# Cross-attention's product with the values, in 64-column blocks per head

## The reference, cut to what matters

```
x = x + xattn(layernorm(x), ctx)          # 64 batches x 64 queries, 256 keys each, 16 heads of 64
    q, k, v = x @ Wq, context @ Wk, context @ Wv
    sim  = einsum('bhid,bhjd->bhij', q, k) * SCALE
    attn = softmax(sim)
    out  = einsum('bhij,bhjd->bhid', attn, v)      # the product with the values
    return out @ Wo + bo
x = x + attn(layernorm(x))                # self-attention, causal
x = x + moe(layernorm(x))                 # 8 experts, top 2
```

## Time and profile before

| | |
|---|---|
| median of 3 runs | 2512.0 us (2511.35 to 2512.2) |
| the profiled execution, its own time | 2510.75 us |
| its span, first to last instruction | 2509.0 us, so 1.75 us lie around it |
| PE busy | 2347.6 us, 94% |
| PEld busy | 2076.7 us, 83% |
| DVE busy | 1589.8 us, 63% |
| ACT busy | 1314.9 us, 52% |
| POOL busy | 903.4 us, 36% |
| granted TensorE clock, mean | 0.978 |
| cross-attention | up to about 1366 us |
| self-attention | about 1405 to 2010 us |
| experts | the rest |

### The profile page before, as it was taken

The page is one execution under the profiler, slowest core; times in us unless marked ns, Lnnn a source line. Parts: engine busy times, 40 slices in busy tenths (PEclk is TensorE's granted clock), DMA queues, the critical chain, the costliest instruction groups (busy, mean ns, idle before and its releaser), DMA issues. The chain is left out here.

```text
span 2509.0 us, 49491 instructions
## 1 busy us (share of the span) xinstructions
PE 2347.6 (94%) x16096; PEld 2076.7 (83%) x16096; DVE 1589.8 (63%) x3452; ACT 1314.9 (52%) x3960; POOL 903.4 (36%) x1141
## 2 busy tenths in 40 slices
PE   6999999999999999999997999999999956888895
PEld 5898889888988898889886899999999844777775
DVE  5656665666566656665655788888888855334332
ACT  4555555555555555555554666666666622333332
POOL 3233333333233323333332122222222224777774
PEclk9999999999999999999999999999999986999998
DMA  5000000000000000000001000000000012334334
GB/s 166 18 10 17 8 17 8 17 9 16 8 17 14 11 8 17 16 9 9 16 1 66 3 10 18 17 8 17 17 8 17 18 37 67 77 73 97 72 49 97
DMA packets 52931, 73.89 MB, mean 29 GB/s; under 512 B 9408, under 2 KB 36800, under 8 KB 52800
## 3 DMA queue, kind: packets, MB, share of 16 engines
q1 hardware_dynamic: 39952, 55.07, 6.9%
q0 software_dynamic: 12912, 17.98, 4.4%
HBM read 55.47 MB, written 21.76 MB: 31 GB/s over the span
## 5 line engine op out<-in xcount | busy, mean ns | idle before, releaser
L356 POOL TENSOR_TENSOR p_sb<-p_sb,rinv 128x512 f32<-128x512 f32 x256 | 284.1, 1110 | 906.3 <-DVE rinv L606 906.3
L527 ACT ACTIVATE p_sb<-s_ps,nmax 128x256 f32<-128x256 f32 x512 | 238.3, 470 | 467.1 <-DVE nmax L587 441.4
L751 POOL TENSOR_TENSOR sp_sb<-sp_sb,srinv 128x512 f32<-128x512 f32 x128 | 133.4, 1042 | 442.7 <-DVE srinv L937 442.7
L462 PE MATMUL o_ps<-pt_sb,v_sb 128*128 128x128 f32 x2048 | 270.5, 275 | 1.8 <-DVE ot_lo L57 1.8
L58 DVE SCALAR_TENSOR_TENSOR qbd_lo<-m_ps,qbd_hi 64x256 fp32r<-64x256 f32 x256 | 108.1, 422 | 227.4 <-ACT qbd_hi L46 225.7
L462 PEld LDWEIGHTS o_ps<-pt_sb,v_sb 128*128 128x128 f32 x2048 | 248.7, 192 | 2.2 <-issue 2.2
L57 DVE TENSOR_TENSOR kt_lo<-k_ps,kt_hi 128x512 fp32r<-128x512 f32 x256 | 176.2, 688 | 98.1 <-ACT kt_hi L45 94.1
L45 ACT CAST kt_hi<-k_ps 128x512 fp32r<-128x512 f32 x256 | 150.6, 588 | 105.7 <-PE k_ps L65 102.7
L885 ACT ACTIVATE sp_sb<-sm_sb,snmax 128x128 f32<-128x128 f32 x512 | 199.4, 390 | 6.6 <-DVE snmax L948 3.3
L603 DVE COPY pt_sb<-t_ps 128x512 f32<-128x512 f32 x256 | 176.4, 689 | 26.5 <-PE t_ps L449 21.8
L587 DVE TENSOR_REDUCE nmax<-s_ps 128x2 f32<-128x512 f32 x256 | 174.1, 680 | 0.0
(11 more groups left out here) (278 smaller groups left out, 7711.3 us busy)
## 6 DMA issues: line engine op xcount, KB each, us to landing
ctx_raw<-in_ctx_t SPq DMA_DIRECT2D x32, 256.0 KB, 2.8
ctx_raw<-in_ctx_t SPq DMA_DIRECT2D x64, 128.0 KB, 2.9
xn<-f_xn SPq DMA_DIRECT2D x16, 256.0 KB, 2.2
acc<-x_sb SPq DMA_DIRECT2D x16, 256.0 KB, 2.3
e_raw<-in_gate SPq DMA_DIRECT2D x8, 512.0 KB, 4.1
e_raw<-in_up SPq DMA_DIRECT2D x8, 512.0 KB, 5.0
e_raw<-in_down SPq DMA_DIRECT2D x8, 512.0 KB, 6.3
x_sb<-in_x SPq DMA_DIRECT2D x1, 3584.0 KB, 13.6
```

The source lines that it names most:

```text
L356: nc.gpsimd.tensor_tensor(prob, prob, inv, ALU.mult).then_inc(norm_done, 1)
L462: mm = pe.matmul(o_ps[:, (2 * w + b) * P:(2 * w + b + 1) * P], v_sb[:, k, q * P:(q + 1) * P], pt_sb[:, w, k * P:(k + 1) * P], start=(j == ...
L527: ex = nc.scalar.activation(p_sb[:, k, b * J:(b + 1) * J], s_ps[1 - w][:, b * J:(b + 1) * J], ACT.Exp, bias=nmax[:, k, b:b + 1], scale=1.0 ...
L751: nc.gpsimd.tensor_tensor(prob, prob, inv, ALU.mult).then_inc(norm_done, 1)
```

## The change

Each of the four fp32 matmuls of a step becomes two, one per head h. The weights are that head's 64 columns of v_sb, the moving operand that head's 64 columns of pt_sb, and the result goes to that head's 64 partitions and to 64 columns of o_ps. The result is dense: two steps fill columns 0 to 255 of o_ps on all 128 partitions. ACT and DVE then read it with one instruction of 128 partitions each, `diag` goes away, and the counts on ot_hi_done follow.

```
-                                    mm = pe.matmul(o_ps[:, (2 * w + b) * P:(2 * w + b + 1) * P],
-                                                   v_sb[:, k, q * P:(q + 1) * P], pt_sb[:, w, k * P:(k + 1) * P],
-                                                   start=(j == 0), stop=(j == 1))
+                                    for h in range(2):
+                                        mm = pe.matmul(o_ps[h * HEAD:(h + 1) * HEAD, (2 * w + b) * HEAD:(2 * w + b + 1) * HEAD],
+                                                       v_sb[:, k, q * P + h * HEAD:q * P + (h + 1) * HEAD],
+                                                       pt_sb[:, w, k * P + h * HEAD:k * P + (h + 1) * HEAD],
+                                                       start=(j == 0), stop=(j == 1))
...
-            def diag(h, w):
-
-                r = slice(h * HEAD, (h + 1) * HEAD)
-                return o_ps[r, :].rearrange("p (k q) -> p k q", k=4)[:, :, h * HEAD:(h + 1) * HEAD]
-
-            def ot_part(ot, h, q):
-                r = slice(h * HEAD, (h + 1) * HEAD)
-                return ot[r, q - 1:q + 1, :].rearrange("p a (b q) -> p (a b) q", b=2)
+            def ot_part(ot, q):
+                return ot[:, q - 1:q + 1, :].rearrange("p a t -> p (a t)")
...
-                            for h in range(2):
-                                split_hi_act(nc, ot_part(ot_hi, h, (p - 4) % PAIRS), diag(h, w)).then_inc(ot_hi_done, 1)
+                            split_hi_act(nc, ot_part(ot_hi, (p - 4) % PAIRS), o_ps[:, 0:2 * P]).then_inc(ot_hi_done, 1)
...
-                            dve.wait_ge(ot_hi_done, PAIRS * t + p - 3)
+                            dve.wait_ge(ot_hi_done, PAIRS // 2 * t + (p - 3) // 2)
                             q = (p - 4) % PAIRS
-                            for h in range(2):
-                                lo = split_lo_dve(nc, ot_part(ot_lo, h, q), diag(h, w), ot_part(ot_hi, h, q))
-                            lo.then_inc(ot_done, 1)
+                            split_lo_dve(nc, ot_part(ot_lo, q), o_ps[:, 0:2 * P], ot_part(ot_hi, q)).then_inc(ot_done, 1)
```

## The result

The changed kernel takes 2471.5 us (median, 2470.0 to 2472.7) against 2512.1 us before, a ratio of 0.9837 with a 95% interval of 0.982 to 0.9854. That is 40.6 us less. The forecast was 2486 us, with bounds of 2475 to 2497, so the sign was right, the size was not, and the time lies under the lower bound.

What follows compares the result with a forecast made beforehand. Cross-attention was taken as bound by TensorE's own stream. Its shorter groups (-25.3 us) and the relief of ACT and DVE (-1 us) made -26 us, from a median of 2512.0 to 2486 us, bounds 2475 to 2497.

Steps and rivals of the forecast that it cites:

- Parts 1 and 2: Line 462, cross-attention: both heads' blocks run side by side as pairs; switching form at both group ends takes 0.505 us.
- Part 3: Line 462's stretch per step: 0.505 + 7 x 0.058 = 0.911 us, 0.099 less than before; -25.3 us over 256 steps.
- Part 4: Reading o_ps with fewer ACT and DVE instructions counts only where TensorE waits for them: -1 us, -5 at most.
- Part 5: TensorE reaches 58 places with a waiting load 0.1 us earlier, giving back up to 6 us; nothing was taken.
- A: Line 462: a floor per matmul makes 64-column pairs pace like 128-column ones; 2582 us, slower; 15 in 100.
- B: Line 462: short loads and matmuls don't overlap fully, pace 0.065 to 0.082 us; 2499 to 2530 us; 16 in 100.
- C: Group ends cost less, or ACT and DVE's relief removes the loads' waits: -35 to -45 us; 5 in 100.

Runs made afterwards that it cites:

- experiment 4: Changed kernel, but with 128 moving columns, the result in its old place and the old two instructions on ACT and DVE; 2568.9 us, ratio 1.0237 to before.
- experiment 5: Changed kernel, but batch 0's four matmuls issued ahead of the transposes and batch 1's behind, so two groups per step; 2539.4 us, ratio 1.0102 to before.
- experiment 6: Changed kernel, but products of two steps issued together in the odd steps, 128 groups instead of 256; 2440.5 us, ratio 0.9725 to before.
- experiment 1: Changed kernel, but ACT and DVE each read the dense result in two instructions of 64 partitions; 2495.1 us, ratio 0.9941 to before.

## Why the prediction was right or wrong

**What bounds the part.** "The stretch is bound by TensorE's own stream ... what ACT and DVE save is not on this path" was wrong. TensorE was busy for 98.9% of the stretch, but a busy time that is the union of overlapping, modelled records hides waits of up to 0.16 us each and shortens the longer ones. The lengths of the steps, 5.50 and 5.17 beside 5.08 and 4.36, were in the same trace and show 25 us of lateness where the waits of TensorE's matmuls add to under 10.

**Parts 1 and 2, pairs and switches.** Right in kind and in size. The pair is concurrent at 64 columns too, the pace is 0.0585 us for 0.058, the ends cost about what line 816's cost (experiments 4, 5 and 6). One sign failed: behind the group the loader's idle time is 0.07 us, not 0.17 to 0.19, though the next matmul comes nearly when it was forecast.

**Part 3, the sum.** Right in kind, a little large: a step lost 0.08 us, not 0.099, so 20.5 us, not 25.3. The stretch measures 0.925 us after, for 0.911 forecast: 0.003 of it is the pace, seven times 0.0005, and 0.011 the two ends. Before, it measures 1.007, read as 1.01. Of the 20.5 only 13.3 (alone) or 14.8 (with the readers' part) reached the end.

**Part 4, ACT and DVE.** This is the step that failed. It was sized at -1 us, "-5 at the very most", and measured 22.0 us on top of the blocks and 20.5 alone. DVE's part is 18.6 of the 22.0 and 19.6 of the 20.5, the rest lies in the drain. The busy time was right (54 us forecast as 53 on DVE), the claim about who waits for it was not. The gains of two places were capped by the idle time in the earlier trace rows, and the chain that makes those waits was not followed.

**Part 5, what is late next.** The +6 us for waits that a faster TensorE uncovers is borne out by experiment 1, where 7 of 20.5 us were lost so. But "between -5 and +6 I take nothing" set it against the relief of part 4, whose bound of 5 us was a quarter of what came.

**The rivals.** A is refuted by the pace. B did not occur. C, "a larger gain" by relief of ACT and DVE, is what happened, with 5 in 100; its two causes were named as one, and only the relief is real, the ends having cost about the same as in self-attention. That its "about 2472 us" lies so close to 2471.5 is luck: no sum stands behind it.

## What to carry to other kernels

Before calling an engine the bound, compare the lengths of like steps over a whole period: a step longer than its twin holds a wait, whatever the busy share says. Follow the loop through the other engines (here DVE, ACT and back, 5.57 to 5.94 us in three steps on end against TensorE's 5.08) and not their busy share; what is saved on it counts where it is late (here 19 of 54 us), and an equal one beside it counted nothing here outside the drain.

Small blocks that run side by side pay at each entry and exit, so put as many as possible into one group. Experiment 6 gained about as much as the change itself (36.5 us of cross-attention beside 35.3) by halving the number of groups.

## What the runs showed of the hardware

Two blocks of 64 weight columns side by side, in plain fp32 with 64 moving columns, pace at 0.0585 us per pair of rows, about half of the 0.109 to 0.111 us with 128 columns, with no sign of a floor at this size. A pair of switches costs 0.30 to 0.35 us of TensorE's time over what the same work would take without. The Trainium skill, "TensorEngine Tiling (Array Packing)", section Key Properties, says that a change of tiling mode drains the engine; the 0.17 us of idle loader ahead of each of 256 groups agree with it. An ot_lo instruction on DVE took 0.423 us on 128 partitions and 0.422 on 64.
